# Attention and feed-forward of one adaLN layer: the order of TensorE's value and ones products, and a feed-forward stage written out unit by unit

## What is computed

```python
h = _layernorm(x) * (1 + ca) + sa
q, k, v = layernorm(h) @ Wq + bq, ... @ Wkv + bkv       # 16 heads of 32
qn, kn = layernorm(rotary(q)), layernorm(rotary(k))
scores = qn @ kn.T / sqrt(32), causal
x = x + ga * (softmax(scores) @ v @ Wo + bo)
h = _layernorm(x) * (1 + cb) + sb
gated = silu(h @ w_gate.T) * (h @ w_up.T)               # 512 -> 2048
x = x + gb * (gated @ w_down.T)                         # 2048 -> 512
```

## Time and profile before

| what | value |
|---|---|
| median of 3 runs | 2559.57 us (2557.92 to 2560.83) |
| the profiled execution's own time | 2558.22 us |
| its span, first to last instruction | 2556.4 us |
| mean granted TensorE clock | 0.964 |
| PE / PEld / DVE / ACT / POOL busy | 92% / 66% / 46% / 31% / 29% |
| attention, about | 443 to 1300 us |
| feed-forward, about | 1466 to 2556 us |

### The profile page before, as it was taken

One profiled execution on the slowest core, in us unless ns is written; L12 is line 12 of the kernel. 1 busy time (PEld: TensorE's weight loads), 2 busy tenths in 40 slices (PEclk: granted clock), 3 DMA queues, 4 the chain that ended last, 5 costly groups with the idle time before them and its releaser, 6 DMA issues. The chain is left out here.

```text
span 2556.4 us, 33412 instructions
## 1 busy us (share of the span) xinstructions
PE 2351.2 (92%) x12504; PEld 1699.5 (66%) x12504; DVE 1178.3 (46%) x1806; ACT 787.0 (31%) x1659; POOL 752.0 (29%) x822
## 2 busy tenths in 40 slices
PE   2899995599999999999958799999999999999998
PEld 0677774466566566556436578787878787878787
DVE  4799996545555555555349721212121212121212
ACT  1333331054454545544535511111111111111111
POOL 1477776001211111121156322222222222222221
PEclk7899997589999999999989999999999999999999
DMA  5122222636545544643058721212121121212111
GB/s 181 59 99 99 98 90 104 140 76 146 122 102 126 134 110 108 140 118 89 19 172 295 259 83 31 87 33 78 38 66 49 45 70 45 70 46 69 41 59 36
DMA packets 162516, 244.80 MB, mean 96 GB/s; under 512 B 17205, under 2 KB 84373, under 8 KB 161902
## 3 DMA queue, kind: packets, MB, share of 16 engines
q1 hardware_dynamic: 153898, 222.23, 30.0%
q0 software_dynamic: 7456, 18.07, 2.6%
q10 hardware_dynamic: 1064, 3.18, 0.3%
HBM read 133.28 MB, written 59.28 MB: 75 GB/s over the span
## 5 line engine op out<-in xcount | busy, mean ns | idle before, releaser
L820 DVE TENSOR_REDUCE b_top<-b_psA 128x2 f32<-128x1024 f32 (+3 forms) x384 | 363.4, 957 | 289.6 <-PE b_psA L739 165.7
L887 ACT ACTIVATE b_probT<-b_psB 128x512 f32<-128x512 f32 (+3 forms) x768 | 339.7, 491 | 349.4 <-PE b_psB L763 234.0
L1227 DVE TENSOR_TENSOR f_gu<-f_psU,f_silu 128x512 f32<-128x512 f32 x128 | 88.5, 691 | 749.3 <-PE f_psU L1288 749.3
L760 PE MATMUL b_psB<-b_stack 98*128 98x512 f32 (+3 forms) x768 | 288.0, 414 | 6.3 <-ACT b_probT L887 4.9
L739 PE MATMUL b_psA<-b_stack 96*128 96x512 f32 (+3 forms) x768 | 256.6, 392 | 28.6 <-DMA b_stack<-b_halves 20.3
L760 PEld LDWEIGHTS b_psB<-b_stack 98*128 98x128 f32 x768 | 140.1, 189 | 190.1 <-issue 118.5
L57 POOL TENSOR_TENSOR f_spots<-f_still 1x1 f32<-1x1 f32 x128 | 25.9, 202 | 795.1 <-PE f_psD L1276 788.8
L1217 ACT ACTIVATE f_silu<-f_psG 128x512 f32<-128x512 f32 x128 | 76.6, 598 | 523.5 <-PE f_psG L1288 523.5
L1274 PE MATMUL f_psD<-f_wd_hi,f_gu_hi 128*128 128x512 f32 x512 | 201.1, 393 | 22.8 <-DVE f_gu_lo L1231 12.3
L1286 PE MATMUL f_psG<-f_hT_hi,w_hi 128*128 128x512 f32 x512 | 200.4, 391 | 11.1 <-DVE f_hT_lo L1238 11.1
L1276 PE MATMUL f_psD<-f_wd_hi,f_gu_lo 128*128 128x512 f32 x512 | 200.0, 391 | 0.0
(11 more groups left out here) (165 smaller groups left out, 4229.0 us busy)
## 6 DMA issues: line engine op xcount, KB each, us to landing
b_stack<-b_halves SPq DMA_DIRECT2D x192, 256.0 KB, 5.0
f_wd<-in_wd_t SPq DMA_DIRECT2D x128, 256.0 KB, 2.6
qkv_d<-a_t SPq DMA_DIRECT2D x32, 512.0 KB, 2.6
b_land<-qkv_d SPq DMA_DIRECT2D x32, 512.0 KB, 4.7
a_x<-in_x SPq DMA_DIRECT2D x32, 256.0 KB, 3.2
qkv_d<-a_v SPq DMA_DIRECT2D x32, 256.0 KB, 2.9
b_v<-qkv_d SPq DMA_DIRECT2D x16, 512.0 KB, 5.8
att_d<-b_att SPq DMA_DIRECT2D x16, 512.0 KB, 3.2
```

Of the source, the lines that this page charges most:

```text
L760: mm = pe.matmul(psB[:, i % 2, cols], stack[0:NR, n % BUFS, 0, j, kb * P:(kb + 1) * P], stack[0:NR, n % BUFS, 1, j, first * P:(half + 1) * ...
L820: dve.tensor_reduce(out, slot("score", NI * n + i)[:, :, 0:width], AX.X, ALU.max, negate=True).then_inc(s["maxed"], 1)
L887: act.activation(probT[:, (NW * n + w) % 3, j, 0:width], psB[:, i % 2, 0:width], ACT.Exp).then_inc(s["expd"], 1)
```

## The change

On TensorE in the attention stage, a step has two halves: shifts 0 and 1, score item 0 and the value products; then shifts 2 and 3, score item 1, `prepare` and `turn_peaks` where there are any, and the ones products. No other engine's order in this stage is touched.

The feed-forward stage is written out for all 128 units, without a loop. `hT_hi` and `hT_lo` get two buffers, so that block i+1 is split in units 8 to 11 of block i, one piece in each. Every down product has a lag of two units. `scaled` gets four buffers: in unit 1 of the next block DVE makes the four `scaled`, in unit 2 the four additions; in the last block the two alternate, and each tile waits only for its own down product (`down_t`). `x1` now lies in the landing buffer of the tokens (`land`), so x1 is loaded once that buffer is split and the next tokens once the outputs are stored. The small instructions behind waits are gone.

```diff
@@ attention_stage, tensor @@
                     if score_at(k):
                         n, w = score_at(k)
                         score(n, 2 * w + i)
-                if prep_at(k):
-                    prepare(*prep_at(k))
-                if peaks_at(k) is not None:
-                    turn_peaks(peaks_at(k))
-                if weigh_at(k):
-                    weigh(*weigh_at(k), False)
-                    weigh(*weigh_at(k), True)
+                    if i == 1 and prep_at(k):
+                        prepare(*prep_at(k))
+                    if i == 1 and peaks_at(k) is not None:
+                        turn_peaks(peaks_at(k))
+                    if weigh_at(k):
+                        weigh(*weigh_at(k), i == 1)
...
@@ ffn_stage @@
-        hT_hi = sb("f_hT_hi", [P, KC, T], F32R)
-        hT_lo = sb("f_hT_lo", [P, KC, T], F32R)
+        hT_hi = sb("f_hT_hi", [P, 2, KC, T], F32R)
+        hT_lo = sb("f_hT_lo", [P, 2, KC, T], F32R)
...
-        scaled = sb("f_scaled", [P, 2, DM])
-        x1 = sb("f_x1", [P, 4, DM])
+        scaled = sb("f_scaled", [P, 4, DM])
+        x1 = land[:].rearrange("p t k q -> p t (k q)")
...
@@ sync @@
+            def load_x1(i):
+                sp.wait_ge(s["h_lo"], KC * min(i + 2, NB))
+                at_least(sp, out_done, 64 * i)
...
-            stagger(sp, NB, HC, [(load_h, 0), (load_wd, 8), (store, 12), (load_x1, 14)])
+            load_h(0)
+            for u in range(NU + 3):
+                i, c = u // HC, u % HC
+                if u < NU:
+                    load_wd(u)
+                if c == 2 and 1 <= i <= NB:
+                    store(i - 1)
+                if c == 4 and i < NB - 1:
+                    load_h(i + 1)
+                if c == 12 and i < NB:
+                    load_x1(i)
@@ gpsimd @@
-                pause(nc, pool, spots[:, 0:1], still[:], wd_in[c % 2], i * (16 * HC // 2) + 16 * (c // 2 + 1))
+                pool.wait_ge(wd_in[u % 2], 16 * (u // 2 + 1))
@@ scalar @@
-            stagger(act, NB, HC, [(split_h, 0), (high, 1), (gated, 0)])
+            for k in range(KC):
+                split_h(0, k)
+            for u in range(NU + 1):
+                i, c = u // HC, u % HC
+                if u >= 1:
+                    high(u - 1)
+                if i < NB - 1 and 8 <= c < 8 + KC:
+                    split_h(i + 1, c - 8)
+                if u < NU:
+                    gated(u)
@@ vector @@
-            stagger(dve, NB, HC, [(product, 1), (split_h, 0), (low, 1), (final, 2)])
+            for u in range(NU + 3):
+                i, c = u // HC, u % HC
+                if 1 <= u <= NU:
+                    product(u - 1)
+                    low(u - 1)
+                if i < NB - 1 and 8 <= c < 8 + KC:
+                    split_h(i + 1, c - 8)
+                if c == 1 and 1 <= i <= NB:
                     for t in range(4):
+                        scale(i - 1, t)
+                        if i == NB:
+                            add(i - 1, t)
+                if c == 2 and 1 <= i < NB:
+                    for t in range(4):
+                        add(i - 1, t)
@@ tensor @@
-            stagger(pe, NB, HC, [(down_early, 2), (down_last, 1), (gate_up, 0)])
+            for u in range(NU + 2):
+                if u >= 2:
+                    down(u - 2)
+                if u < NU:
+                    at_least(pe, s["silu"], u - 1)
+                    matrix(u, 0)
+                    at_least(pe, s["gu"], u - 1)
+                    matrix(u, 1)
```

More of the change, by code:

```diff
@@ L1143, in ffn_stage @@
         psD = ctx.enter_context(nc.psum_tensor("f_psD", [P, 4, DM], F32))
-        names = ("gate_in h_in h_hi h_lo gate_mm up_mm silu gu gu_hi gu_lo wd_hi wd_lo down "
-                 "scaled final still").split()
+        x1 = land[:].rearrange("p t k q -> p t (k q)")
+        names = ("h_in h_hi h_lo gate_mm up_mm silu gu gu_hi gu_lo wd_hi wd_lo down down_t "
+                 "scaled final").split()
         s = {n: sem("f_" + n) for n in names}
         wd_in = [sem(f"f_wd_in{j}") for j in range(2)]
+        gate_in = sem("f_gate_in")
         x1_in = sem("f_x1_in")
@@ L1151, in ffn_stage @@
         block = ctx.enter_context(nc.Block())
-        def done(i, c):
-            return i * HC + (c + 1)
         @block.sync
         def _(sp):
[L1158 to L1170, removed]
-                    at_least(sp, s["scaled"], 4 * i)
[L1172 to L1181, removed]
-            stagger(sp, NB, HC, [(load_h, 0), (load_wd, 8), (store, 12), (load_x1, 14)])
@@ new lines, in load_h, with load_wd @@
+            def load_h(i):
+                at_least(sp, s["h_lo"], KC * i)
+                at_least(sp, out_done, 64 * (i - 1))
+                sp.dma_start(land[:], scratch["h2"][i * 4:(i + 1) * 4].rearrange("t p k q -> p t k q")).then_inc(s["h_in"], 16)
+            def load_wd(u):
+                at_least(sp, s["wd_lo"], u - 1)
+                c = u % HC
+                sp.dma_start(wd[:, u % 2], args["wd_t"][c * P:(c + 1) * P, :]).then_inc(wd_in[u % 2], 16)
+            def load_x1(i):
+                sp.wait_ge(s["h_lo"], KC * min(i + 2, NB))
+                at_least(sp, out_done, 64 * i)
+                src = scratch["x1"].ap().rearrange("(i t) p n -> i p t n", t=4)
+                sp.dma_start(land[:].rearrange("p t k q -> p t (k q)"), src[i]).then_inc(x1_in, 16)
+                if i % 2 == 0:
+                    at_least(sp, s["scaled"], 4 * i)
+                    src = scratch["mod"][i // 2:i // 2 + 1, 5, :]
+                    sp.dma_start(gate[:], src.broadcast_to([P, DM])).then_inc(gate_in, 16)
@@ new lines, in store @@
+            def store(i):
+                for t in range(4):
+                    sp.wait_ge(s["final"], 4 * i + t + 1)
+                    sp.dma_start(out[i * 4 + t:i * 4 + t + 1].rearrange("a p n -> p (a n)"), x1[:, t]).then_inc(out_done, 16)
+            load_h(0)
[9 more added lines that the diff above has]
+                    load_x1(i)
@@ L1198, in _ @@
-            stagger(pool, NB, HC, [(split_wd, 0)])
+            for u in range(NU):
+                at_least(pool, s["down"], u - 1)
+                pool.wait_ge(wd_in[u % 2], 16 * (u // 2 + 1))
+                pool.tensor_scalar(wd_hi[:, u % 2], wd[:, u % 2], 1.0, 1.0, ALU.mult, ALU.mult).then_inc(s["wd_hi"], 1)
+                pool.wait_ge(s["wd_hi"], u + 1)
+                pool.tensor_tensor(wd_lo[:, u % 2], wd[:, u % 2], wd_hi[:, u % 2].bitcast(F32), ALU.subtract).then_inc(s["wd_lo"], 1)
@@ L1200, in _, with split_h @@
         @block.scalar
         def _(act):
-            def split_h(i, c):
-                if c == 0:
+            def split_h(i, k):
+                if k == 0:
                     act.wait_ge(s["h_in"], 16 * i + 16)
[L1205 to L1217, removed]
-            stagger(act, NB, HC, [(split_h, 0), (high, 1), (gated, 0)])
+                    at_least(act, s["up_mm"], HC * (i - 1))
+                act.activation(hT_hi[:, i % 2, k].rearrange("p (t q) -> p t q", q=P), land[:, :, k], ACT.Copy).then_inc(s["h_hi"], 1)
@@ new lines, in high, with gated @@
+            def high(u):
+                act.wait_ge(s["gu"], u + 1)
+                at_least(act, s["down"], u - 1)
+                act.activation(gu_hi[:, u % 2], gu[:, u % 2], ACT.Copy).then_inc(s["gu_hi"], 1)
+            def gated(u):
+                act.wait_ge(s["gate_mm"], u + 1)
+                at_least(act, s["gu"], u - 1)
+                act.activation(silu[:, u % 2], psG[:, u % 2], ACT.Silu).then_inc(s["silu"], 1)
+            for k in range(KC):
+                split_h(0, k)
@@ L1229, in low @@
[L1229 to L1244, removed]
-                    for t in range(4):
[L1246 to L1250, removed]
@@ L1252, in _, with split_h, product @@
-            stagger(dve, NB, HC, [(product, 1), (split_h, 0), (low, 1), (final, 2)])
+            def split_h(i, k):
+                dve.wait_ge(s["h_hi"], KC * i + k + 1)
+                whole, hi, lo = land[:, :, k], *[x[:, i % 2, k].rearrange("p (t q) -> p t q", q=P) for x in (hT_hi, hT_lo)]
+                dve.tensor_tensor(lo, whole, hi.bitcast(F32), ALU.subtract).then_inc(s["h_lo"], 1)
+            def product(u):
+                dve.wait_ge(s["up_mm"], u + 1)
+                dve.wait_ge(s["silu"], u + 1)
+                at_least(dve, s["gu_hi"], u - 1)
+                dve.tensor_tensor(gu[:, u % 2], psU[:, u % 2], silu[:, u % 2], ALU.mult).then_inc(s["gu"], 1)
@@ new lines, in low, with scale @@
+            def low(u):
+                dve.wait_ge(s["gu_hi"], u + 1)
+                dve.tensor_tensor(gu_lo[:, u % 2], gu[:, u % 2], gu_hi[:, u % 2].bitcast(F32), ALU.subtract).then_inc(s["gu_lo"], 1)
+            def scale(i, t):
+                if t == 0:
+                    dve.wait_ge(gate_in, 16 * (i // 2 + 1))
+                    at_least(dve, s["final"], 4 * i)
+                if t < 3:
+                    dve.wait_ge(s["down_t"], 3 * i + t + 1)
+                else:
```

(38 more changed lines are left out.)

23 lines of the change are left out of this document (1 added, 22 removed).

## The result

The changed kernel takes 2648.19 us (median of 4 runs, 2644.60 to 2651.49) against 2560.20 before: a ratio of 1.034 with a 95% interval of 1.0318 to 1.0362. It is 88 us slower, where 49 were forecast with a range up to 2634. The sign was right, the size wrong.

The account below looks back on a forecast made before the run. PE was taken to bound both stages. Copy waits +56, split +10, last group -4, clock +18 and feed-forward -30 gave +50 us: 2609 us as a median, 1.9% slower, range 2578 to 2634.

Parts of the forecast that it names:

- The wait for the copy: Attention: value products wait for DVE's copy of psO, 14 times 2.14 us and 15 times 1.76 us, +56 us.
- The split: Attention: two bursts per step cost 39 us in exits and entries, avoided waits give back 29 us; net +10 us.
- the last group: Attention's last 12 steps, without items between shifts: value products fill waits for exponentials, -4 us (0 to -8).
- The feed-forward stage: Both PE waits at each block change go, along with a clock fall, and the end starts sooner; -30 us.
- The clock: Attention: PE drops to 1.2 GHz after a third of the 29 new waits, 10 falls at 1.8 us, +18 us.
- the clock falls at most waits: Rival, attention: clock cost of 45 us in place of 18, total 2636 us; chance 0.10.
- the prediction's own end of 29 falls: Attention: upper end of the clock term, a fall at all 29 added waits, 52 us.
- signs of being wrong: Copy waits at L836 staying near nothing, or the feed-forward stage not shrinking by 26 to 30 us.
- no wait would appear: Rival, attention: DVE's copy is done before PE arrives, so 56 and 18 us go; 2536 us, chance 0.07.
- the clock never falls: Rival, attention: the waits stand but PE keeps full clock; 2591 us, inside the forecast's range, no chance of its own.
- the split is free: Rival, attention: a second exit costs nothing, -29 in place of +10; 2571 us, near 2553 if the clock holds; chance 0.06.
- the feed-forward stage wins nothing: Rival, feed-forward: a new wait on SP's queue cancels the gain; 2639 us, chance 0.03.

Follow-up runs that it names:

- e4: The changed kernel, with 7 or 6 extra matmuls on PE in each of the 29 steps where it waits for the copy; 2590.13 us, ratio 1.0113.
- e3: The changed kernel, with DVE copying psO ahead of the first score item's maximum; 2539.34 us, ratio 0.9916.
- e2: The kernel before with the new feed-forward stage alone; 2532.10 us, ratio 0.9886.
- e1: The kernel before with the new order of TensorE's attention step alone, feed-forward stage still a loop; 2678.28 us, ratio 1.046.
- e7: The changed kernel, with the value products behind shifts 2 and 3, ahead of item 1, in the 29 steps with a copy; 2589.97 us, ratio 1.0116.
- e9: The changed kernel, with 3 extra matmuls on PE in each of the 29 waits for the copy; 2599.73 us, ratio 1.0158.
- e6: The kernel before with the new feed-forward stage, old order on PE, and DVE's copy ahead of the first item's maximum; 2529.75 us, ratio 0.9877.

## Why the prediction was right and wrong

- **The wait for the copy: right.** Forecast were 29 waits, 2.14 and 1.76 us each, 56 us together, in place of 15 short ones. The trace has 29 waits of 2.0 and 1.7 us, 54.1 in total, and the time that they cost apart from the clock is 50.8 us (e4 against e3, where 3.7 us of waits for the copy are left).
- **The split: right.** Net +10 and -4 for the last group were forecast, +6 together, with the 15 old waits for the copy taken as gone; e3 against e2 measures +7.2. By the traces of these two, the stretch from the first to the last score item takes 790.3 us against 779.5 (+10.9), what follows it 43.5 against 48.1 (-4.6). One thing the sum left out is in them: PE waits for DVE's maximum at a score slot 21 times for 10.3 us in e3, 8 times for 7.1 in e2. The timeline of PE after, in the steps that answer to the earlier trace rows, shows both sides of it:

```profile
720.29 0.73 PE L760 MATMUL b_psB<-b_stack 98*128 98x512 f32 x2
720.86 0.62 PE L739 MATMUL b_psA<-b_stack 96*128 96x512 f32 x2
721.41 1.07 PE L778 MATMUL b_psO<-b_probT,b_v 128*32 128x512 f32 x8
722.40 0.73 PE L760 MATMUL b_psB<-b_stack 98*128 98x512 f32 x2
722.97 0.28 PE L739 MATMUL b_psA<-b_stack 96*128 96x256 f32 x1
...
723.48 1.06 PE L778 MATMUL b_psL<-b_probT,b_ones 128*32 128x512 f32 x8
724.47 0.50 PE L760 MATMUL b_psB<-b_stack 98*128 98x512 f32 x1
```

  Shifts 2 and 3 take 0.57 us (722.40 to 722.97) where they took 0.83, so their waits are gone. Each burst takes 0.99 us to the next shift, 1.98 for two where one of both took 1.85 (745.07 to 746.92): the 0.13 of the forecast. The step takes 4.18 us against 4.37. The rule of the Trainium skill (TensorE: Matmul & The Clock Gate, "Step-by-step: what each phase is for"), by which the weights of a next tile load under the last one's matmul, would by the prediction's costing have made e3 some 40 us faster than it is; for these bursts the trace doesn't agree, with the 0.13 us above. That it is the weight load that costs this time isn't shown.
- **The feed-forward stage: right.** -30 were forecast, e2 measures -30.2. From first to last matmul the stage takes 1046.7 us in place of 1075.3, and the stretch behind the last matmul 6.2 in place of 8.0. That leaves little room for a hold-up by the loads that share a buffer now, or for a cost of writing out 128 units. DVE's last chain, against the earlier trace rows, begins ahead of PE's last matmul (2641.25 at its end):

```profile
2639.35 0.69 DVE L1254 TENSOR_TENSOR f_scaled<-f_psD,f_gate 128x512 f32<-128x512 f32 x1 [1.42 <-PE f_psD L1292]
...
2644.34 0.69 DVE L1259 TENSOR_TENSOR f_land<-f_land,f_scaled 128x512 f32<-128x512 f32 x1
```

- **The clock: wrong, and the step that failed.** "I take a third, 10 falls: +18 us." The runs showed 24 falls and 58 us, 40 us more than the term; the total was missed by 39. The mechanism was named, both of its factors were too small. The four measured terms, 58.1 for the clock, 50.8 for the waits, 7.2 for the split and -30.2 for the feed-forward stage, make +85.9, against 88 in all. The number of falls: I took it from the feed-forward stage, where 1 of 14 waits was followed by a fall, and only raised it for sparser work by feel; in attention 2.0 us were enough 14 times in 14, and 1.5 us 9 times in 13. The price: the 1.8 us came from the one fall there, which ended after 3.4 us; here more than half lasted twice as long, and a fall costs 2.4 us on average. The rival "the clock falls at most waits" had the right count in view, 25 falls, but with 45 us and a chance of 0.10 it was priced and weighed too low. The range ended at 2634, though the prediction's own end of 29 falls (52 us) gives 2643 with the sum's other terms. And what it named as signs of being wrong covers the waits and the feed-forward stage, not the clock.
- **The other rivals.** That no wait would appear is excluded by the 29 waits of the trace, that the clock never falls by the 24 falls (e4, where it doesn't, takes 2590.1 us, and that rival stood at 2591), that the split is free by e3, and that the feed-forward stage wins nothing by e2.

Why waits of the same length bring more falls in attention (19 of 30 of 1.7 us) than in the feed-forward stage (1 of 14 of 1.8) stays open. That attention's work is sparser was argued and not tested. Nor was it tried to fill PE's waits in the other stages.

## What to carry to other kernels

Before moving an instruction forward on the bounding engine, look up what it waits for, and what stands ahead of that in the other engine's queue: here a copy behind a maximum turned an order that costs 7 us into one that costs 116, and moving the copy by one place mends it. A short idle stretch of TensorE that recurs is to be priced with the fall of the clock that it can bring, which here cost more than the waits; where such a stretch can't be avoided, extra matmuls into a buffer that is overwritten anyway can win time, as they did here. And decide an interleaving step by step: it pays where it covers a wait and costs an exit and an entry where there is none.

## What was not expected of the hardware

- The clock fell at idle stretches of TensorE shorter than this kernel's feed-forward stage suggested. Of the waits for the copy in the attention stage it fell at 28 of 28 of 2.0 us and 19 of 30 of 1.7 (the kernel after and e1), at 9 of 13 of 1.5 (e7), 4 of 15 of 1.3 (e9, e7), and none of 30 of 0.8 and 1.0 us. In the feed-forward stage it fell at 1 of 14 waits of 1.8 us (the kernel before and e1) and none of 14 of 1.5. Twice it fell in the last group with only idle stretches under 0.5 us just before (e6, e7).
- The falls aren't the same in every execution: over the same attention order and the same waits, the kernel after has 24 with 129.7 us at the lower level, e1 has 23 with 119.5. e7's four executions have mean granted clocks from 0.956 to 0.961, and the one with 0.956 is the slowest.
- Extra matmuls on a TensorE that waits anyway shortened the kernel: 188 of them took 58 us off (e4).
- Going into and out of the four column tiles costs about 0.2 us a time (0.09 in and 0.09 out, from the starts in the earlier trace rows), and the busy rows don't show it: e3's window is busy for 98.94 us of 100 with 738 matmuls, e2's for 98.89 with 745.
